# A graph network's edge sort: the norm of H by four chunks, a wait per sort operation, weights first on ScalarE

## What is computed

```python
h = jnp.maximum(_layernorm(x, axis=-1), 0.0)
x = x + _L0_gnn_ref(h, ...)   # edge softmax over relu(h[src]) + 1e-7, then a two-layer perceptron
h = jnp.maximum(_layernorm(x, axis=-1), 0.0)
x = x + _L1_gnn_ref(h, ...)   # two linear layers with batch norm over [h[src], h[dst]], segment sum
h = jnp.maximum(_layernorm(x, axis=-1), 0.0)
x = x + _L2_gnn_ref(h, ...)   # two spline convolutions
h = jnp.maximum(_layernorm(x, axis=-1), 0.0)
x = x + _L3_gnn_ref(h, ...)   # three rounds of relu(x[src] + edge term), segment sum, linear
```

## Time and profile before

| | |
|---|---|
| timed runs, median of 3 | 8522.31 us |
| lowest, highest | 8464.91, 8526.42 us |
| profiled execution, its own time | 8603.34 us |
| its span | 8601.5 us, 40281 instructions |
| mean granted TensorE clock | 0.686 |

### The profile page before, as it was taken

One profiled execution on the slowest core, in us unless ns is written; L12 is line 12 of the kernel. 1 busy time (PEld: TensorE's weight loads), 2 busy tenths in 40 slices (PEclk: granted clock), 3 DMA queues, 4 the chain that ended last, 5 costly groups with the idle time before them and its releaser, 6 DMA issues. The chain is left out here.

```text
span 8601.5 us, 40281 instructions
## 1 busy us (share of the span) xinstructions
PE 2740.4 (32%) x8087; PEld 1662.7 (19%) x8087; DVE 4029.2 (47%) x7722; ACT 1558.9 (18%) x2650; POOL 5181.1 (60%) x5117
## 2 busy tenths in 40 slices
PE   0000000013323300228663555577433344444322
PEld 0000000011211100003221333355322222222111
DVE  9869558941344510016543666576566322222111
ACT  0000001200111100117552111122244111111000
POOL 7747734774467577760445565466477566566566
PEclk9999999975555555559876666677655555565555
DMA  1101100112322000111111222223244233233111
GB/s 48 31 17 24 25 14 15 27 45 55 99 45 47 10 23 23 16 16 39 45 45 36 45 45 45 39 52 53 57 91 89 51 55 52 46 53 55 45 44 38
DMA packets 429273, 365.19 MB, mean 42 GB/s; under 512 B 123103, under 2 KB 399108, under 8 KB 428663
## 3 DMA queue, kind: packets, MB, share of 16 engines
q0 software_dynamic: 163392, 77.79, 10.2%
q1 hardware_dynamic: 245868, 256.09, 9.5%
q10 hardware_dynamic: 19786, 28.92, 1.0%
HBM read 206.39 MB, written 158.75 MB: 42 GB/s over the span
## 5 line engine op out<-in xcount | busy, mean ns | idle before, releaser
L918 POOL DMA_INDIRECT g_ring<-tab,QB x784 | 755.7, 964 | 464.6 <-issue 234.8
L918 POOL DMA_INDIRECT c_ring<-tab,QB x784 | 781.1, 996 | 419.0 <-issue 221.8
L1595 PE MATMUL c_psU<-spline,c_hzT 97*128 97x288 f32 x1568 | 643.7, 569 | 335.1 <-DVE c_V L1550 228.4
L918 POOL DMA_INDIRECT nodes_ring<-nodes,b_own x320 | 312.5, 977 | 538.6 <-DMA x2d_lin<-nodes_ring 438.6
L918 POOL DMA_INDIRECT l_ring<-in_x_dram,a_own x392 | 446.9, 1140 | 314.4 <-POOLq L102 195.2
L918 POOL DMA_INDIRECT l_ring<-agg_tab,QA x392 | 396.7, 1012 | 335.4 <-POOLq L102 178.2
L918 POOL DMA_INDIRECT c_ring<-nodes,b_other x392 | 386.2, 985 | 282.8 <-issue 128.7
L918 POOL DMA_INDIRECT H<-xe_tab,idx_a x392 | 413.2, 1054 | 217.6 <-issue 119.2
L2224 POOL DMA_INDIRECT out_dram<-out_rowr,out_idxr x392 | 385.9, 985 | 196.6 <-issue 124.1
L918 POOL DMA_INDIRECT rows_b<-b_edges,idx_b x392 | 410.5, 1047 | 144.7 <-issue 119.4
L1595 PEld LDWEIGHTS c_psU<-spline,c_hzT 97*128 97x128 f32 x1568 | 398.0, 271 | 503.0 <-issue 326.4
(11 more groups left out here) (544 smaller groups left out, 8079.7 us busy)
## 6 DMA issues: line engine op xcount, KB each, us to landing
tab<-c_rows SPq DMA_DIRECT2D x147, 128.0 KB
nodes<-l_decay ACTq DMA_DIRECT2D x40, 322.3 KB
nodes_x<-nodes SPq DMA_DIRECT2D x50, 257.8 KB
c_din<-dst_lin SPq DMA_DIRECT2D x98, 128.0 KB
c_ring<-tab SPq DMA_DIRECT2D x98, 128.0 KB
c_ring<-tab,QB POOLq DMA_INDIRECT x784
dst_lin<-c_yd SPq DMA_DIRECT2D x98, 128.0 KB
g_din<-dst_lin SPq DMA_DIRECT2D x98, 128.0 KB
```

Of the source, the lines that this page charges most:

```text
L918: pool.indirect_dma_start(out=ring[:, at + j, :], out_offset=None, in_=table, in_offset=bass.IndirectOffsetOnAxis(ap=idx[:, w:w + 1], axis ...
L1595: ins = pe.matmul(self.psU[i % 2][:, t, 0:288], self.hzT[c % 2][:, (2 * i + t) * P:(2 * i + t + 1) * P], w[:, :, :].rearrange("p o j -> p ...
```

## The change

Three edits in `order_edges` and what it calls. H is normed in groups of four chunks: 12 groups of four and one of one, with tiles of [128, 32] and [128, 32, 32], one tile for the squares instead of two; `centre` waits for all chunks of a group and, after its last reduce, for that reduce; each operation waits for the one before. In the network, the join's forward pass and its way back, every `link.inc` of a group with one wait at its end becomes a `link`. `weights.load` is called right behind ScalarE's two copies, before the wait for `decoded`, and the bias rows of the spline weights are loaded by one DMA per convolution, not nine.

```diff
@@ Weights.__init__
-            for j in range(9):
-                loads.append((self.raw[c][3 * D:3 * D + 1, j, :], bias.unsqueeze(0)))
+            loads.append((self.raw[c][3 * D:3 * D + 1, :, :], over(bias.unsqueeze(0), 1, 9)))
@@ Network.vector
-                link.inc(v.tensor_scalar(lo, lo, self.even[0:SR, :], None, ALU.mult))
-                link.inc(v.tensor_scalar(up, up, self.odd[0:SR, :], None, ALU.mult))
-                v.wait_ge(link.sem, link.base + link.n)
+                link(v.tensor_scalar(lo, lo, self.even[0:SR, :], None, ALU.mult))
+                link(v.tensor_scalar(up, up, self.odd[0:SR, :], None, ALU.mult))
...
-                    link.inc(v.tensor_copy(C[1][q], whole(X[at])[r]))
+                    link(v.tensor_copy(C[1][q], whole(X[at])[r]))
                     if riding:
-                        link.inc(v.tensor_copy(CW[1][q], whole(XW[at])[r]))
-                v.wait_ge(link.sem, link.base + link.n)
+                        link(v.tensor_copy(CW[1][q], whole(XW[at])[r]))
...
-            link.inc(v.transpose(C[0], whole(X[at])))
+            link(v.transpose(C[0], whole(X[at])))
             if riding:
-                link.inc(v.transpose(CW[0], whole(XW[at])))
-            v.wait_ge(link.sem, link.base + link.n)
+                link(v.transpose(CW[0], whole(XW[at])))
...
@@ Join.forward
-        link.inc(v.memset(X[0][:, 0, :], 300000.0))
-        link.inc(v.memset(X[0][:, 1, :], -1.0))
-        link.inc(v.memset(flat2(XW[0]), 0.0))
-        v.wait_ge(link.sem, link.base + link.n)
+        link(v.memset(X[0][:, 0, :], 300000.0))
+        link(v.memset(X[0][:, 1, :], -1.0))
+        link(v.memset(flat2(XW[0]), 0.0))
...
@@ Join.back
-            link.inc(v.tensor_tensor(x, lo, d, ALU.add))
-            link.inc(v.tensor_tensor(y, hi, d, ALU.subtract))
-            v.wait_ge(link.sem, link.base + link.n)
+            link(v.tensor_tensor(x, lo, d, ALU.add))
+            link(v.tensor_tensor(y, hi, d, ALU.subtract))
...
@@ order_edges
-    NR, NE = 4, 3
+    NR, NE, NG = 4, 3, 4
+    groups = [range(i, min(i + NG, g.NCH)) for i in range(0, g.NCH, NG)]
...
             act.copy(table[:, :, 4:12], raw8).then_inc(rows_made, 1)
+            weights.load(act)
             act.wait_ge(decoded, 1)
...
-            weights.load(act)
             act.wait_ge(joined, 1)
...
-            for c in range(g.NCH):
-                norm_act(g, act, act_in, act_out, c + 1, CH, t[c % 2])
+            for q, cs in enumerate(groups):
+                norm_act(g, act, act_in, act_out, q + 1, len(cs) * CH, t[q % 2])
...
+            def centre(q):
+                b, cs = t[q % 2], groups[q]
+                n = len(cs) * CH
+                h = H[:, cs[0] * CH:cs[0] * CH + n, :]
+                for c in cs:
+                    v.wait_ge(agot[c % NR], 16 * CH * (c // NR + 1))
+                link(v.tensor_reduce(b.s[:, 0:n], h, AX.X, ALU.add))
+                link(v.tensor_scalar(b.s[:, 0:n], b.s[:, 0:n], -1.0 / D, None, ALU.mult))
+                link(v.tensor_tensor(b.xc[:, 0:n, :], h, over(b.s[:, 0:n], 2, D), ALU.add))
+                link(v.tensor_tensor(sq[:, 0:n, :], b.xc[:, 0:n, :], b.xc[:, 0:n, :], ALU.mult))
+                v.tensor_reduce(b.var[:, 0:n], sq[:, 0:n, :], AX.X, ALU.add).then_inc(act_in, 1)
+                v.wait_ge(act_in, q + 1)
+
+            def scale(q):
+                b, cs = t[q % 2], groups[q]
+                n = len(cs) * CH
+                h = H[:, cs[0] * CH:cs[0] * CH + n, :]
+                v.wait_ge(act_out, q + 1)
+                link(v.reciprocal(b.rs[:, 0:n], b.sd[:, 0:n]))
+                for c in cs:
+                    v.wait_ge(akept[(c // 2) % 2], 16 * (c // 4 + 1))
+                link(v.scalar_tensor_tensor(h, b.xc[:, 0:n, :], 0.0, over(b.rs[:, 0:n], 2, D), ALU.max, ALU.mult))
+                link(v.tensor_scalar(h, h, 1e-7, None, ALU.add))
+            for q in range(len(groups)):
+                centre(q)
+                if q:
+                    scale(q - 1)
+            scale(len(groups) - 1)
```

More of the change, by code:

```diff
@@ L355, in vector @@
                 at = 1 - at
-            link.inc(v.transpose(whole(X[1]), C[at]))
+            link(v.transpose(whole(X[1]), C[at]))
             if riding:
-                link.inc(v.transpose(whole(XW[1]), CW[at]))
-            v.wait_ge(link.sem, link.base + link.n)
+                link(v.transpose(whole(XW[1]), CW[at]))
             at = 1
@@ L417, in forward @@
         C, CW = [flat2(t) for t in n.C], [flat2(t) for t in n.CW]
-        link.inc(v.memset(X[0][:, 0, :], 300000.0))
-        link.inc(v.memset(X[0][:, 1, :], -1.0))
-        link.inc(v.memset(flat2(XW[0]), 0.0))
-        v.wait_ge(link.sem, link.base + link.n)
[L422 to L426, removed]
+        link(v.memset(X[0][:, 0, :], 300000.0))
+        link(v.memset(X[0][:, 1, :], -1.0))
+        link(v.memset(flat2(XW[0]), 0.0))
+        link(v.tensor_scalar(X[0][0:SR, 0, :], key[:, 0, :], 2.0, None, ALU.mult))
+        link(v.tensor_scalar(X[0][0:SR, 1, :], key[:, 1, :], 2.0, 1.0, ALU.mult, ALU.add))
+        link(v.tensor_scalar(XW[0][0:SR, 0, :], slot[:, :], 1.0, None, ALU.add))
+        link(v.tensor_scalar(XW[0][0:SR, 1, :], slot[:, :], -1.0, -1.0, ALU.mult, ALU.add))
         pair = lambda t: (t[:, 0, :], t[:, 1, :])
@@ L432, in forward @@
             for q, r in zip(near, far):
-                link.inc(v.tensor_copy(C[1][q], flat2(X[at])[r]))
-                link.inc(v.tensor_copy(CW[1][q], flat2(XW[at])[r]))
-            v.wait_ge(link.sem, link.base + link.n)
+                link(v.tensor_copy(C[1][q], flat2(X[at])[r]))
+                link(v.tensor_copy(CW[1][q], flat2(XW[at])[r]))
             for q, r in zip(near, far):
@@ L440, in forward @@
             at = 1 - at
-        link.inc(v.transpose(C[0], flat2(X[at])))
-        link.inc(v.transpose(CW[0], flat2(XW[at])))
-        v.wait_ge(link.sem, link.base + link.n)
+        link(v.transpose(C[0], flat2(X[at])))
+        link(v.transpose(CW[0], flat2(XW[at])))
         at = 0
@@ L450, in forward @@
             at = 1 - at
-        link.inc(v.transpose(flat2(X[1]), C[at]))
-        link.inc(v.transpose(flat2(XW[1]), CW[at]))
-        v.wait_ge(link.sem, link.base + link.n)
+        link(v.transpose(flat2(X[1]), C[at]))
+        link(v.transpose(flat2(XW[1]), CW[at]))
         at = 1
@@ L544, in back @@
             for q, r in zip(near, far):
-                link.inc(v.tensor_copy(far_[q], flat2(XW[at])[r]))
-            v.wait_ge(link.sem, link.base + link.n)
+                link(v.tensor_copy(far_[q], flat2(XW[at])[r]))
             for q, r in zip(near, far):
@@ L620, in order_edges @@
         for i in range(2):
-            t[i].s, t[i].var, t[i].sd, t[i].rs = (ph.sb(f"ln_{n}{i}", [P, CH]) for n in ("s", "var", "sd", "rs"))
-            t[i].xc, t[i].sq = ph.sb(f"ln_xc{i}", [P, CH, D]), ph.sb(f"ln_sq{i}", [P, CH, D])
+            t[i].s, t[i].var, t[i].sd, t[i].rs = (ph.sb(f"ln_{n}{i}", [P, NG * CH]) for n in ("s", "var", "sd", "rs"))
+            t[i].xc = ph.sb(f"ln_xc{i}", [P, NG * CH, D])
+        sq = ph.sb("ln_sq", [P, NG * CH, D])
         space = H[:, :, :].rearrange("p w f -> p (w f)")
@@ L803, in _ @@
                 flag_segments(g, v, link, K[i], F, before[i], after[i], edged, 16 * 4)
[L805 to L824, removed]
@@ L825, in _ @@
-            scale(g.NCH - 1)
-            v.wait_ge(chain, link.n)
+            def centre(q):
[10 more added lines that the diff above has]
+                v.wait_ge(act_in, q + 1)
```

## The result

Over 20 runs each, the changed kernel has a median of 8492.6 us (8444.6 to 8694.0), the kernel before 8527.5 us (8464.9 to 8593.8). The ratio is 0.9941, 95% interval 0.9917 to 0.9966: 50 us less, where 39 were forecast. That ratio leaves out runs over 1.5% above the fastest of their kernel, and for once they can't be passed over: they are six of the changed kernel's 20, at 8626 to 8694 us, and none of before's. The other 14 lie between 8445 and 8542. The median of all 20 is 35 us lower than before's; their mean is not lower at all, 8532.7 against 8532.8. So the change has two faces: 50 us gained in most runs, 116 us lost in three of ten.

A forecast was written before the change was run, and what follows sets the result against it. The prediction took VectorE's chain of first sort, join, second sort and norm to bound the first phase. Its terms, -44.3 + 5 + 0 = -39 us, gave 8483 us against the median of 8522.3, range 8465 to 8505.

The forecast's parts named there:

- Part 1: Norm of H on VectorE, four chunks at a time: 137.3 us become 93.0, 44.3 us less.
- upper bound of 47: Norm of H in groups: with no gap between instructions, 47 us less.
- gathers don't become the bound: End of the first phase: the last gather is issued at 1175.45, before the norm begins, so VectorE's norm still ends last.
- Part 2: A wait for each operation in the sorts and join: 44 neighbours at 0.11 us, 5 us taken, bounds 0 and 15.
- Part 3: Weights issued first on ScalarE, 161 DMA issues instead of 177: taken as 0, between 73 us gained and 78 lost.
- Directly this is worth 0: Early weights on ScalarE: issues end near 120 to 202, its next task is at 357.91, so no time gained directly.
- I take 0, by the stretch in which ScalarE does nothing: Early weights' indirect effect on VectorE: 0, since from 928 to 1190 VectorE is as slow with ScalarE idle.
- Rival A: ScalarE's issues slow VectorE in the join; moving them gains 73 us at most, 8410, or 8445 if half; chance 0.20.
- Rival B: VectorE's slow pace follows an amount of issued DMA work, reached near 105 us; 142 us more, 8625; chance 0.10.
- Rival C: VectorE reaches the norm before H has arrived; the gain is 13 us instead of 44, 8514; chance 0.12.
- The join done near 644 to 650: Sign of a right forecast: VectorE has joined the two sorted orders near 644 to 650 us.
- the second sort's end near 1220: Sign of a right forecast: VectorE ends the second sort, ahead of the norm, near 1220 us.

The follow-up runs named there:

- norm-only kernel: The kernel before with only the norm of H changed, to groups of four chunks; 8489.8 us, ratio 0.9956.
- gap kernel: The changed kernel, but ScalarE issues the weights only when GpSimd's first gathers have been stored; 7064.3 us, ratio 1.0007, on a quick chip; later 0.9996 on another.
- weights alone: The kernel before with only the weights' load changed: ScalarE issues it, in 161 DMAs, at the head of its program; 8623.2 us, ratio 1.0047.
- waits only: The kernel before with one edit: in the sorts each operation waits for the one ahead of it; 8530.9 us, ratio 0.9978.
- norm and waits: The changed kernel with the weights back at their old place behind the first sort; 8471.0 us, ratio 0.9933.

## Why the prediction came out right, and where it was thin

The forecast median was 8483, the measured one 8492.6, and that it came so near is in part luck. The ratio's interval, 29 to 71 us less, takes in 39, but it speaks of 14 runs of 20, and the mean of all is no gain. By stages even those 14 gain less than 50 us: the norm-only kernel, which is before's code ahead of the norm, begins its norm at 1192.1, and with before's own 139.7 us behind that the next phase would begin at 1331.8; in the changed kernel it begins at 1302.6, 29 us earlier (an estimate from three profiles).

**Part 1** carried it. Forecast -44.3 us; measured -42.9 from the norm's first operation to its last (137.3 to 94.4), and -43.5 in the mean of the runs with this edit alone. Its terms hold to 0.02 us, apart from the reciprocal (0.20 taken, 0.353 measured); its upper bound of 47 adds up to 47.8 with its own terms. The statement "gathers don't become the bound" holds on the slow chip and fails on the quick ones.

**Part 2**, 5 us taken. On the slow chip it is under the spread. On the quick chips, where stages repeat closely, it is clean: the first sort ends 0.7 us later and the join takes 3.4 us more (205.9 to 209.3), the same in the gap kernel, where the weights aren't early; this goes with the 8 and 30 neighbours at 0.11 counted for them. The Trainium skill (VectorE: DVE Perf Modes, The DRAIN you can't avoid) would have 0; the measurement decides for 4.

**Part 3**, 0 taken, is the step that was thin. "Directly this is worth 0" holds (the issues end at 157.6, inside 120 to 202). "I take 0, by the stretch in which ScalarE does nothing" doesn't: that stretch shows that a crawl needs no ScalarE, which isn't the same as that ScalarE can't bring one on. The early issues cost 27 us in the first sort and give back 17 in the join at best. In six of 20 runs the kernel lands 166 us above its others (8649 against 8483, the two means), with weights alone in six of 12 it lands 107 above, and such a group is missing in the 85 runs of before, norm only, waits only, and norm and waits, whose highest is 8611. So the early weights bring it on; by what mechanism is not shown, and the profile of the weights-only kernel is the only trace of such a run.

**Rival A** (relief): refuted as the cause. With ScalarE silent the changed kernel still crawls from 400 to 553; some 17 of its 73 us are real: between 400 and 553 VectorE is busy 97.5 us there, and 79.6 to 82.0 us in the norm-only, waits-only and norm-and-waits kernels, in which ScalarE issues the weights in that stretch. **Rival B** (slower): its price was 142 us; seen were 107 and 166 between the two groups of runs and 155 at the phase's end in the one profile. Its sign in the trace, starts 1.4 apart before 250, is there. Its chance of 0.10 was a third of the share of runs it struck, and its trigger was wrong: by 50 us GpSimd and ScalarE had issued 78 of the 205 DMAs it asked for, while the waits-only kernel went past 270 gathers unslowed. Neither an amount nor a time sets the onset. **Rival C** (norm bound by gathers): absent here, and the whole truth on the quick chips, where the gain is 0, not 13.

"The join done near 644 to 650" (634.2) and "the second sort's end near 1220" (1193.8, start of its last operation, 1219.4 before) missed since they were built on before's profile, whose crawl began at 290 where the other profiles' began near 400.

What makes a chip slow is not settled. Between its two profiles the kernel before loses 1533 us, 256 in this phase and the rest later; in this phase every slowed stretch begins where GpSimd gathers. It outlasts them: in the second stage of all six slow profiles by 15 to 18 us (in before's the last gather is issued at 1175.5, the pace ends at 1194), in the first stage of the weights-only profile by 14. The Trainium skill (SBUF — State Buffer, SBUF: two separate sides) has VectorE and GpSimd exclude each other by a shared port pair, for certain pairs of operations, for a whole instruction. The quick chips run the same pairs with VectorE 95% busy, so here that rule alone can't be the cause, nor does it explain a pace that outlasts the gathers. An untested rival is that something feeds several engines too slowly, the supply of instructions for one: in the crawl VectorE's starts mostly lie one or two steps of 0.70 us apart, and ScalarE's issues take 0.70 us as well.

## What to carry to other kernels

Work taken off one engine is worth its time only as long as no other engine ends just behind it: ask which transfer ends next, and by how much. A burst of DMA issues is not free because its own engine idles. On the slow chip it did no such harm at its old place behind the first sort; a place without gathers was timed on quick chips alone. And look at all the runs and not only at their median, as a cost that strikes in three of ten hides in a spread. Where a stage crawls in a way that no wait in the trace explains, run the kernel on another chip before building on it.

## What the runs showed of the hardware

- One kernel took 8539 us on one chip and 7062 to 7075 on three (one job each), with the granted TensorE clock at 0.68 and 0.70. The page of before on a quick chip, VectorE and GpSimd in slices of 177 us, against the earlier trace rows:

```profile
DVE  9999998982344620046755887787676233233111
...
POOL 7777777787777677777677776775776776776677
```

- In the slow pace VectorE mostly starts one instruction every 1.40 us, whether it takes 0.43 us (before, 935 to 1176) or 0.69 (weights only). GpSimd doesn't slow beside it: from 170 to 400 it does 170 instructions in the weights-only profile and 165 in the changed kernel's, where VectorE isn't slowed. Nor are the two in lockstep: in before, from 935 to 1176, gathers start 1.25 us apart in the median. The pace began at 290 or at 400 us in the same code, and at 50 with the early weights.
- ScalarE's DMA issues for `we` take 0.70 us in the median beside gathers on the slow chip, and 0.28 on a quick one beside the same gathers.
